# Attention maxima: the negation is taken out, minus ones stand beside the stacked keys, and the partial maxima get two buffers

## What is computed

```python
q = (x @ Wq + bq).reshape(B, N, NUM_HEADS, HEAD_DIM)
k = (y @ Wk + bk).reshape(B, M, NUM_HEADS, HEAD_DIM)
v = (y @ Wv + bv).reshape(B, M, NUM_HEADS, HEAD_DIM)
scores = jnp.einsum('bnhd,bmhd->bhnm', q, k) * scale
attn = jax.nn.softmax(scores, axis=-1)
out = jnp.einsum('bhnm,bmhd->bnhd', attn, v).reshape(B, N, IMAGE_DIM)
```

## Time and profile before

| What | us |
|---|---|
| median of 3 runs | 3046.11 (3045.59 to 3048.97) |
| the profiled execution, its own time | 3049.87 |
| its span | 3048.0 |
| TensorE matmul busy | 2937.2 (96%) |
| GpSimd busy | 2022.4 (66%) |
| VectorE busy | 2250.0 (74%) |
| ScalarE busy | 1682.5 (55%) |
| mean granted TensorE clock | 0.988 of full |

### The profile page before, as it was taken

The page is one execution under the profiler, slowest core; times in us unless marked ns, Lnnn a source line. Parts: engine busy times, 40 slices in busy tenths (PEclk is TensorE's granted clock), DMA queues, the critical chain, the costliest instruction groups (busy, mean ns, idle before and its releaser), DMA issues.

```text
span 3048.0 us, 39906 instructions
## 1 busy us (share of the span) xinstructions
PE 2937.2 (96%) x14712; PEld 1804.6 (59%) x14712; DVE 2250.0 (74%) x3368; ACT 1682.5 (55%) x2920; POOL 2022.4 (66%) x745
## 2 busy tenths in 40 slices
PE   7999999999999999999999999999999887899999
PEld 4666666666666666666666666666534333344477
DVE  7777777777777777777777777777746899986653
ACT  1566666666666666666666666666641555321021
POOL 1699999999999998999999999999950000000000
PEclk9999999999999999999999999999999989999999
DMA  6534444454434445443444434443450112214100
GB/s 167 136 81 101 111 110 91 96 118 98 101 88 117 97 122 129 106 114 89 101 101 117 95 91 112 110 102 80 89 194 12 52 54 97 82 56 167 69 14 18
DMA packets 108886, 296.10 MB, mean 97 GB/s; under 512 B 23762, under 2 KB 28882, under 8 KB 99122
## 3 DMA queue, kind: packets, MB, share of 16 engines
q1 hardware_dynamic: 99044, 226.71, 26.6%
q0 software_dynamic: 9072, 66.06, 11.5%
q10 hardware_dynamic: 576, 0.79, 0.1%
HBM read 114.46 MB, written 8.06 MB: 40 GB/s over the span
## 4 chain that ended last, share of the span: by engine, by line
PE 86%; DVE 10%; ACT 1%; issue 1%; DMA 1%; POOL 0%; SPq 0%; ACTq 0%; DVEq 0%; POOLq 0%
PE ps L1828 16%; PE ps L1867 15%; PE ps L1854 14%; PE ps L1781 9%; PE ps L1812 9%; PE ps L1805 8%; PE ps L2077 4%; PE ps L2041 4%; DVE pm L1053 3%; PE ps L2057 3%; PE ps L1884 2%; DVE bx L1315 1%; PE ps L1836 1%; PE ps L2069 1%; ACT V L1523 1%
## 5 line engine op out<-in xcount | busy, mean ns | idle before, releaser
L1053 DVE TENSOR_REDUCE pm<-ps 128x1 f32<-128x512 f32 x2048 | 1408.2, 691 | 523.4 <-PE ps L1828 450.7
L1537 ACT ACTIVATE pf<-ps 128x512 f32<-128x512 f32 x2048 | 1218.8, 600 | 695.5 <-PE ps L1854 610.8
L900 POOL TENSOR_TENSOR psum<-psum,pf 128x2048 f32<-128x2048 f32 x317 | 1455.6, 4592 | 25.2 <-ACT pf L1537 9.0
L1828 PE MATMUL ps<-ks,qs 96*128 96x512 f32 x2048 | 847.8, 414 | 25.1 <-DVE pm L1053 19.8
L1854 PE MATMUL ps<-qs,ks 98*128 98x512 f32 x2048 | 814.2, 399 | 3.4 <-ACT pf L1537 3.3
L1828 PEld LDWEIGHTS ps<-ks,qs 96*128 96x128 f32 x2048 | 387.1, 189 | 291.9 <-issue 201.5
L1867 PE MATMUL ps<-pf,V 128*32 128x512 f32 x4096 | 496.0, 602 | 0.0
L1854 PEld LDWEIGHTS ps<-qs,ks 98*128 98x128 f32 x2048 | 391.2, 191 | 50.1 <-ACT pf L1537 13.0
L915 POOL PARTITION_ALL_REDUCE qstat<-qstat x2 | 0.7, 367 | 605.5 <-DVE qstat L1351 605.5
L900 POOL TENSOR_TENSOR psum<-pf 128x2048 f32<-128x2048 f32 x64 | 303.2, 4738 | 53.5 <-ACT pf L1537 53.5
L1805 PE MATMUL ps<-cTh,Wkg 128*128 128x512 f32 x732 | 292.9, 400 | 2.7
(11 more groups left out here) (224 smaller groups left out, 3029.6 us busy)
## 6 DMA issues: line engine op xcount, KB each, us to landing
ks<-KH SPq DMA_DIRECT2D x512, 128.0 KB, 3.1
psum<-pf POOLq DMA_DIRECT2D x63, 1024.0 KB, 7.8
ks<-KL SPq DMA_DIRECT2D x256, 128.0 KB, 3.1
cT<-in_ctxT SPq DMA_DIRECT2D x32, 768.0 KB, 4.7
Wkg<-wk_rows SPq DMA_DIRECT2D x61, 384.0 KB, 5.5
BC<-bc_rows SPq DMA_DIRECT2D x32, 512.0 KB, 4.8
ring<-in_ffn_w SPq DMA_DIRECT2D x16, 1024.0 KB, 7.8
wA<-in_W_fcT SPq DMA_DIRECT2D x4, 1024.0 KB, 10.1
```

Source lines behind the costliest of these rows:

```text
L900: pool.tensor_tensor(acc, before, pf[:, tile % P_SLOTS, :], ALU.add).then_inc(s_sum, 1)
L1053: dve.tensor_reduce(pm[:, n // BLK, n % BLK:n % BLK + 1], src, AX.X, ALU.max).then_inc(s_wfree, 1)
L1537: act.activation(pf[:, tile % P_SLOTS, j * NTOK:(j + 1) * NTOK], ps[:, S_BANK + u % S_BANKS, :], ACT.Exp, scale=SCALE).then_inc(s_exp, 1)
L1828: last = pe.matmul(dst, qs[0:3 * HD, h, t * P:(t + 1) * P], ks[0:3 * HD, keys_of(of, j), i * 512:(i + 1) * 512], start=True, stop=True)
```

## The change

`nm`, its instruction and its semaphore `s_nm` go. TensorE transposes `mn` itself, and waits for `s_fin` in place of `s_nm`. The two rows beside the stacked keys hold minus ones in place of ones, so that the second product again subtracts the maximum. They are written by the same two memsets, and the copy of them for the third buffer of keys is the same DMA. Since VectorE no longer waits for `s_fin` behind the reduction of `pm`, its next "A" reductions would write to `pm` while it is still being read; so `pm` gets two buffers, used by turns of the group, and GpSimd writes the seed to the buffer of the next group.

```diff
-        s_nm = sem("s_nm")
...
-        pm = sb("pm", [P, HG * NT, BLK + 1], c=att)
+        pm = sb("pm", [P, 2, HG * NT, BLK + 1], c=att)
         mn = sb("mn", [P, HG * NT], c=att)
         dm = sb("dm", [P, HG * NT], c=att)
-        nm = sb("nm", [P, HG * NT], c=att)
...
             for g in range(KS - 1):
-                pool.memset(ks[3 * HD:SROWS, g * HG:(g + 1) * HG, :].bitcast(F32), 1.0).then_inc(s_ones, 1)
+                pool.memset(ks[3 * HD:SROWS, g * HG:(g + 1) * HG, :].bitcast(F32), -1.0).then_inc(s_ones, 1)
...
                     if of // NG == NCH - 1 and g == NG - 1:
-                        pool.memset(pm[:, :, BLK], LOWEST).then_inc(s_seed, 1)
+                        pool.memset(pm[:, (of + 1) % 2, :, BLK], LOWEST).then_inc(s_seed, 1)
                     else:
                         n = (of + 1) % NG
-                        pool.tensor_copy(pm[:, :, BLK], m_run[:, n * HG * NT:(n + 1) * HG * NT]).then_inc(s_seed, 1)
+                        pool.tensor_copy(pm[:, (of + 1) % 2, :, BLK], m_run[:, n * HG * NT:(n + 1) * HG * NT]).then_inc(s_seed, 1)
...
-            dve.memset(pm[:, :, BLK], LOWEST)
+            dve.memset(pm[:, 0, :, BLK], LOWEST)
...
-                    dve.tensor_reduce(pm[:, n // BLK, n % BLK:n % BLK + 1], src, AX.X, ALU.max
+                    dve.tensor_reduce(pm[:, of % 2, n // BLK, n % BLK:n % BLK + 1], src, AX.X, ALU.max
...
-                dve.tensor_reduce(mn[:], pm[:], AX.X, ALU.max).then_inc(s_fin, 1)
-                dve.wait_ge(s_fin, of + 1)
-                dve.tensor_scalar(nm[:], mn[:], -1.0, None, ALU.mult).then_inc(s_nm, 1)
+                dve.tensor_reduce(mn[:], pm[:, of % 2], AX.X, ALU.max).then_inc(s_fin, 1)
...
-                    pe.wait_ge(s_nm, x[1] + 1)
-                    last = pe.transpose(dst[0:HG * NT, 0:P], nm[:], ident[:])
+                    pe.wait_ge(s_fin, x[1] + 1)
+                    last = pe.transpose(dst[0:HG * NT, 0:P], mn[:], ident[:])
```

## The result

The changed kernel takes 3053.87 us (median of 22 runs, 3047.23 to 3060.98) against 3048.64 (22 runs, 3045.59 to 3051.65) beside it: a ratio of 1.0019, 95% interval 1.0012 to 1.0025. It is slower by about 5 us where 12 us less were forecast.

The account below looks back on a forecast made before the run. TensorE was taken to bound attention, with some 23 us idle. Removed stalls of 16.8 us less 5.0 given back to key waits left 11.8 us net, forecasting a median of 3034.3 us, range 3028.5 to 3041.5.

Parts of the forecast that it names:

- The stall: `nm` on VectorE held up under GpSimd's running add in 29 of 64 groups; removing it gains TensorE 16.8 us.
- The 13 small ones: Stalls of `nm` in 13 groups at position 2, such as group 14: 0.66 us each, 8.5 us together.
- Position 3 costs nothing: Stalls of `nm` in 13 groups at position 3 hide under TensorE's wait for stacked keys: 0 us.
- the slope of the keys' wait: Stacked keys at position 3: as TensorE gets earlier, 0.3 us new wait per us, 2.6 us over 13 chunks.
- 13 plain chunks: Key waits at position 3 following the 13 smaller position 2 stalls: 0.2 us new wait each, 2.6 us given back.
- rival 1: Key waits take back all small gains, slope 1 per us: gain 5.9 us, 3040.2 us; chance 0.12.
- group 36: Its keys' issue, 3.95 us behind GpSimd's, stretches to 9.5 us; no wait now, 1.6 us new wait forecast (0 to 3.2).
- the two large stalls: Stalls of `nm` in groups 34 and 2: gains of 4.8 and 3.5 us, with 1.6 and 0.8 given back.
- The clock: TensorE's granted clock falls after idle over 1.8 us, as in groups 2 and 34; no new falls in the sum.
- rival 4: Slower: key waits at position 3 stretch to over 1.8 us and the clock falls, 3067 us; chance 0.02.
- GpSimd costs nothing: GpSimd has less idle, but ScalarE's exponentials don't begin to wait for its sums: no cost.

Follow-up runs that it names:

- the last experiment: Changed kernel with GpSimd's rescale of the output moved ahead of its transfer into the sums, so the transfer is issued later: 3074.76 us, ratio 1.0083.

## Why the prediction was wrong

- **The stall** was right in cause, place and price. The 13 small ones were worth 8.7 us against 8.5: 0.67 each, where I had 0.39 of idle plus 0.27. Up to the transposes of groups 2 and 34 the gains were 2.9 and 2.8 us against 2.9 and 3.2.
- **Position 3 costs nothing** was right for this kernel: the wait for keys hid the stall, and taking that wait away brought it out. I did not say that the change was then worth more than 16.8 us as soon as the keys were early.
- **The step that failed is the slope of the keys' wait**, "From 2.3 to 1.65 I take 0.3 per us". From the rows I read a curve that flattens. But rows 10 and 11 alone have the issues stretched by 3.2 us for 3.3 us of earlier start, a slope of 0.97, and the measurement has 1. In the 13 plain chunks the stacking starts 2.27 us behind the transfer's issue before and 1.56 after, and the keys land 15.27 and 15.28 us behind that issue. The landing is tied to the transfer, so TensorE waits as much longer as it arrives earlier: the bound I gave to rival 1. The row of group 36 that bent my curve was a single case, with the start of the stacking and GpSimd's lateness both out of the ordinary.
- So the waits for keys grew from 10.3 us (17.5 in the earlier trace rows and 2.6 that the profile puts down to issue, less 9.8 that stood at stalls) to 24.1, by 13.8 us instead of 5.0. The 13 plain chunks give 9.3 of it, where I had 2.6. At the two large stalls I gave back 1.6 and 0.8; group 35 now idles 2.12 us, where it had no idle time, and group 3 for 2.92 us where it was 0.54, which is beyond the bound of 1.6 that I had set. (My "about 13 to 14 us" of waits in the changed profile doesn't follow from my own terms either: 10.3 + 5.0 is 15.3.)
- **The clock** was only in rival 4, as all or nothing at 1.8 us of idle, and the sum put it at nothing. Waits of 1.4 to 1.9 us now stand in most chunks, and two of them are followed by a fall (groups 11 and 15, at 1.63 and 1.87 us). The changed kernel's profile has 4 falls in steady attention (behind the maxima of groups 3, 35, 11 and 15), before had 2 (groups 2 and 34). Those two are 2.3 of the 16.8 us, so without the clock the change gains 14.5 us and gives back 13.8. That leaves a gain of 0.7, where the medians show a loss of 5.2: some 6 us are left for the clock.
- The mean granted clock of the 22 runs is 0.9859, that of the 27 runs of before beside the experiments 0.9885. The difference, 0.0026 of the span, is 8 us at most, enough for the 6. Among the 22 runs of the changed kernel alone, the three with a clock of 0.988 take 3051.1 us on average and the nine with 0.985 take 3056.1. That the clock makes up all of the 6 us is worked out from these means, not shown by a run of its own: in the profiled execution the four falls are worth 6.8 us, so that the terms give a loss of 3.8 (16.8 - 13.8 - 6.8), and from the transpose of group 1 to that of group 63 it is 1.3. It was rivals 1 and 4 together, which I had treated as separate. I had given the slower side 0.02.
- The step that **GpSimd costs nothing** held: no exponential waits for its sums.

What stays open is why the clock falls behind some waits of 1.6 us and more and not behind others, and why the transfer holds up the stacking to a fixed time and not by a share.

## What to carry to other kernels

Before a stall is taken out, find what the released engine will meet next and what that thing's time is tied to. If it is tied to an engine that doesn't get earlier, the gain can be returned there in full, as here; the price is read from the landing behind its cause, over all instances, and not from three rows. Two waits that hide one another are worth little singly and much together, so such edits are tried as a pair. And a wait that all of a tile's copies must satisfy can often be split by what the first consumer really reads.

## What the runs showed of the hardware

- A `TENSOR_SCALAR` of 128x16 in f32 from SBUF to SBUF is held up until GpSimd's running `TENSOR_TENSOR` has ended (up to 3.33 us for 0.17 us of work): in the four traces that have it, all 118 long ones end 30 to 45 ns behind such an add. A `TENSOR_REDUCE` of the same data with `negate` takes 0.170 or 0.171 us in all 64 cases, 31 of them under an add.
- A software DMA of 1024 KB that adds into SBUF delays 12 copies of 128 KB on SyncE's queue until they land 15.3 us behind its issue on average (14.9 to 15.8), whether they start 2.3 or 1.6 us behind it; in the last experiment, where they start 1.2 us behind it, it is 15.9. At 256 KB they land 12.0 us behind it before the change (11.6 to 13.3) and 11.9 after (11.3 to 12.6).
- Over the nine traces of this case, in steady attention, none of 119 idle times of TensorE between 0.25 and 1.4 us was followed by a fall of the clock, 2 of 15 between 1.4 and 1.8 us were, and 23 of 29 longer ones. A fall with TensorE at work behind it cost about 1.7 us, as in the earlier trace rows; 6 of the 25 were twice as long.
